# Zero matmuls in TensorE's early gaps, expert numbers read earlier, rows sent a turn sooner, result loads from two queues

## What is computed

```python
x = x + attention(layernorm(x), ln1_g, ln1_b, Wq, Wkv, Wo, ln2_g, ln2_b)   # x: (4, 512, 128)
x = x + experts(layernorm(x), gate_w, gate_up_w, down_w)

# attention: 16 query heads of 64, one key and one value head that all share
xn = layernorm(x) * ln1_g + ln1_b
q, k, v = xn @ Wq, xn @ Wk, xn @ Wv
attn = softmax(q @ k.T * 64 ** -0.5)
y = layernorm(concat_heads(attn @ v) @ Wo) * ln2_g + ln2_b

# experts: 8 of them, the best 2 of each token, 512 hidden features
probs = softmax(x @ gate_w.T);  topw, sel = top_k(probs, 2);  topw = topw / sum(topw)
out = sum over the 2 chosen e of  topw[e] * ((up_e(x) * gelu(gate_e(x))) @ down_w[e].T)
```

## Time and profile before

| | |
|---|---|
| median of 3 runs | 633.98 us (633.31 to 635.54) |
| the profiled execution, its own time | 634.79 us |
| its span, first to last instruction | 633.0 us |
| TensorE busy with matmuls | 575.8 us, 91% |
| VectorE busy | 422.4 us, 67% |
| GpSimd busy | 391.3 us, 62% |
| ScalarE busy | 303.7 us, 48% |
| mean granted clock of TensorE | 0.965 |

### The profile page before, as it was taken

The page is one execution under the profiler, slowest core; times in us unless marked ns, Lnnn a source line. Parts: engine busy times, 40 slices in busy tenths (PEclk is TensorE's granted clock), DMA queues, the critical chain, the costliest instruction groups (busy, mean ns, idle before and its releaser), DMA issues. The chain is left out here.

```text
span 633.0 us, 8708 instructions
## 1 busy us (share of the span) xinstructions
PE 575.8 (91%) x2559; PEld 324.4 (51%) x2559; DVE 422.4 (67%) x815; ACT 303.7 (48%) x570; POOL 391.3 (62%) x319
## 2 busy tenths in 40 slices
PE   2799999999999999979999989899997989899990
PEld 1354454444554454445544544444442567788880
DVE  3777558658847978686587767977485868344433
ACT  2235655445545554354556434355544654455540
POOL 4338686658668855598597556959755934355330
PEclk9889999999999999789999978999998999999995
DMA  6121011010101100061000000000006200231005
GB/s 173 47 88 69 2 68 69 0 69 0 70 16 53 69 1 1 5 250 47 1 1 1 2 1 15 17 6 0 10 1 167 64 22 27 53 97 36 21 14 199
DMA packets 23980, 29.28 MB, mean 46 GB/s; under 512 B 4403, under 2 KB 14901, under 8 KB 23936
## 3 DMA queue, kind: packets, MB, share of 16 engines
q1 hardware_dynamic: 21664, 24.50, 11.9%
q0 software_dynamic: 2272, 4.24, 2.0%
HBM read 13.73 MB, written 15.32 MB: 46 GB/s over the span
## 5 line engine op out<-in xcount | busy, mean ns | idle before, releaser
L1059 ACT ACTIVATE prob<-s_ps 128x512 f32<-128x512 f32 x256 | 150.6, 598 | 191.5 <-PE s_ps L1152 189.5
L985 DVE TENSOR_REDUCE rowmax<-max_ps 128x1 f32<-128x512 f32 x256 | 173.1, 685 | 90.1 <-PE max_ps L1121 88.4
L922 POOL TENSOR_TENSOR fold<-prob 128x1024 f32<-128x1024 f32 x63 | 149.6, 2374 | 96.7 <-ACT prob L1059 96.2
L1166 PE MATMUL pv_ps<-prob,v 128*64 128x512 f32 x512 | 140.4, 628 | 0.0
L1150 PE MATMUL s_ps<-q_hl,khh 128*128 128x512 f32 x256 | 119.3, 466 | 1.5 <-DMA q_hm<-mrow 0.9
L1121 PE MATMUL max_ps<-khh,q_hl 128*128 128x512 f32 x256 | 106.0, 422 | 9.0 <-DVE q_hl L974 4.4
L1152 PE MATMUL s_ps<-q_hm,kly 65*128 65x512 f32 x256 | 102.9, 402 | 0.0
L1150 PEld LDWEIGHTS s_ps<-q_hl,khh 128*128 128x128 f32 x256 | 49.3, 193 | 81.7 <-ACT prob L1059 58.1
L928 POOL TENSOR_TENSOR psums<-fold 128x512 f32<-128x512 f32 x63 | 81.3, 1290 | 4.9
L1121 PEld LDWEIGHTS max_ps<-khh,q_hl 128*128 128x128 f32 x256 | 50.4, 197 | 30.0 <-DVE rowmax L985 10.4
L1152 PEld LDWEIGHTS s_ps<-q_hm,kly 65*128 65x128 f32 x256 | 49.4, 193 | 9.1 <-issue 3.3
(11 more groups left out here) (218 smaller groups left out, 769.9 us busy)
## 6 DMA issues: line engine op xcount, KB each, us to landing
sorted_rows<-raw_w SPq DMA_DIRECT2D x36, 260.0 KB, 2.6
raw_w<-in_gate_upT SPq DMA_DIRECT2D x8, 512.0 KB, 7.6
wd<-in_downT SPq DMA_DIRECT2D x8, 256.0 KB, 4.2
raw_w<-parts SPq DMA_DIRECT2D x8, 256.0 KB, 4.0
psums<-sorted_rows SPq DMA_DIRECT2D x22, 65.0 KB, 1.8
x<-in_x SPq DMA_DIRECT2D x4, 256.0 KB, 5.3
out<-x SPq DMA_DIRECT2D x4, 256.0 KB, 2.7
xs_first<-sorted_rows SPq DMA_DIRECT2D x15, 65.0 KB, 1.9
```

The source lines that it names most:

```text
L922: nc.gpsimd.tensor_tensor(fold[:, :, :], prob[:, head % 4, 0:2, :], prob[:, head % 4, 2:4, :], ALU.add).then_inc(prob_folded, 1)
L985: nc.vector.tensor_reduce(rowmax[:, group % 2, it, i:i + 1], max_ps[:, k % 2, :], AX_X, ALU.max).then_inc(max_done, 1)
L1059: nc.scalar.activation(prob[:, head % 4, jt, :], s_ps[:, k % 2, :], ACT.Exp, scale=SCALE).then_inc(exp_done, 1)
L1166: last = nc.tensor.matmul(pv_ps[DH * hd:DH * hd + DH, :], v[:, b % 2, jt, :], prob[:, head % 4, jt, :], start=(jt == 0), stop=(jt == JT - 1))
```

## The change

Four things are changed.

- **Zeros.** A tile of zeros is cleared by GpSimd as its first step (in the last slot of `q_hm`, which is not used until later), and TensorE multiplies it by itself into `y_ps`, which nobody reads then, at fixed places of the first steps: 20 times at the very start, before the first K 8, before the first MAX 5, before the first EXP 3, before the first V 3, and once before each of the MAX tiles 2 to 11. None of these is followed by a signal.
- **Expert numbers.** TensorE's first three register loads stand ahead of the last row sum in the first block instead of behind the first transpose of the second.
- **Rows.** `SEND_AT` is 9 instead of 10, the turn in which PLACE stands.
- **Result loads.** SyncE issues four of the eight loads, and ScalarE, at the end of its program, the other four; each waits for all results first.

```diff
@@ -130,6 +130,10 @@
+BUSY = {"start": 20, "K": 8, "MAX": 5, "EXP": 3, "V": 3, "rows": 1}
 def shifts(units):
@@ -152,6 +156,9 @@
 EARLY_ROWS = 2
+OPEN = 3
@@ -276,6 +283,7 @@
         half_set = sem("half_set")
+        idle_set = sem("idle_set")
         x1_in = [sem(f"x1_in{b}") for b in range(NB)]
@@ -646,6 +654,12 @@
+        tile_expert = []
+        def load_expert(pe, k):
+            tile_expert.append(pe.value_load(tile_at[0:1, 0, k:k + 1], min_val=0, max_val=E - 1))
         def load_gate_up(sp, e):
@@ -793,6 +807,9 @@
+            idle_rows = q_hm[:, Q_SLOTS - 1, :]
             wq_raw = prob[:, 0, 0:2, :].rearrange("p a s -> p (a s)")
@@ -861,6 +878,7 @@
             def _(pool):
+                nc.gpsimd.memset(idle_rows.bitcast(F32), 0.0).then_inc(idle_set, 1)
                 nc.gpsimd.memset(minus_half[:, :], -0.5).then_inc(half_set, 1)
@@ -1077,10 +1095,20 @@
+                def keep_busy(times):
+                    for _ in range(times):
+                        nc.tensor.matmul(y_ps[:, :], idle_rows[:, 0:P], idle_rows, start=True, stop=True)
+                pe.wait_ge(idle_set, 1)
+                keep_busy(BUSY["start"])
                 pe.wait_ge(consts_in, 96)
                     b = u // 2
+                    if u == 0 and a == 0 and kind in BUSY:
+                        keep_busy(BUSY[kind])
                     if kind in ("XT", "K", "V", "Q", "SHIFT", "YT", "X3T", "LOGIT", "RANK") and (kind, u) != ("K", 0):
@@ -1115,6 +1143,8 @@
                             pe.wait_ge(q_lo, u * UH + i + 1)
+                        if 2 <= k < 12:
+                            keep_busy(BUSY["rows"])
                         if k >= 2:
@@ -1168,6 +1198,11 @@
                             last.then_inc(pv_mm, 1)
+                    if (kind, u, a) == ("SUM", last_unit, 1):
+                        pe.wait_ge(tiles_ready, 1)
+                        for k in range(OPEN):
+                            load_expert(pe, k)
                     tail_tensor(pe, kind, u, a)
@@ -1215,16 +1250,14 @@
-
-            OPEN = 3
             BETWEEN = {"YT": 3, "YSTAT": 3, "YADD": 4, "XSTAT": 4, "XNORM": 5, "X3T": 6, "LOGIT": 6, "CHOOSE0": 6, "CHOOSE1": 7,
-            SEND_AT = 10
+            SEND_AT = 9
             ROW_SENDS = range(SEND_AT, SEND_AT + TOP_K * TPB * 2 // 3 + 1)
-            assert SEND_AT > BETWEEN["PLACE"] and EOW >= TOP_K * TPB + 4
+            assert SEND_AT >= BETWEEN["PLACE"] and EOW >= TOP_K * TPB + 4
@@ -1259,6 +1292,14 @@
                 eng.wait_ge(parts_sent[k % EOW], 16 * (k // EOW + 1))
+            def load_parts(eng, n):
+                for k in range(NT - EOW, NT):
+                    sent(eng, k)
+                for b in range(NB):
+                    eng.dma_start(part_in[:, b, n, :, :], parts[n * T + b * S:n * T + (b + 1) * S, :].rearrange(
+                        "(p t) d -> p t d", t=TPB)).then_inc(parts_in[b], 16)
@@ -1280,12 +1321,7 @@
                         load_rows(sp, k, rows(k))
-                for k in range(NT - EOW, NT):
-                    sent(sp, k)
-                for b in range(NB):
-                    for n in range(TOP_K):
-                        sp.dma_start(part_in[:, b, n, :, :], parts[n * T + b * S:n * T + (b + 1) * S, :].rearrange(
-                            "(p t) d -> p t d", t=TPB)).then_inc(parts_in[b], 16)
+                load_parts(sp, 0)
                 for b in range(NB):
@@ -1435,6 +1471,8 @@
+                load_parts(act, 1)
             @block2.tensor
@@ -1494,10 +1532,6 @@
-                def expert(k):
-
-                    tile_expert.append(pe.value_load(tile_at[0:1, 0, k:k + 1], min_val=0, max_val=E - 1))
-
                 def gate(k):
@@ -1515,10 +1549,7 @@
-                tile_expert = []
                 turn_in(0)
-                for k in range(OPEN):
-                    expert(k)
                 for e in range(E):
```

## The result

The changed kernel takes 629.69 us (median of 20 runs, 623.06 to 635.11) against 634.84 (20 runs, 631.76 to 636.23): 5.1 us or 0.8% less. The prediction said 625.7 with a range of 621.8 to 630.2. The runs of the change spread over 12 us, those of before over 4.5. The profiled execution, 635.11 us with a span of 633.1, is the longest of the 20: its rows show what happened in it, and its total is not typical.

A forecast was written before the change was run, and what follows sets the result against it. No single engine fills the span: attention hands tiles between four engines, TensorE paces the experts' part. Terms 3.1 + 1.0 + 1.0 + 2.9 + 0.3 = 8.3 us gave a 625.7 us median, range 621.8 to 630.2.

The forecast's parts named there:

- part 2: Start of the experts' part: early register loads save TensorE 3.4 us, but GpSimd's late reciprocal leaves 1.0 us.
- rivals of 628.6 and 628.8: Start gives only 1 us and the 42 us spell stays (628.8), or part 3's wait moves (628.6); together chance 0.2.
- the first rival: GpSimd not in the way in part 2, or issue time counts in part 4: 2 us more, 623.5; chance 0.15.
- The fourth rival: Slower: clock falls come elsewhere later; two new spells take back 8.3 us, three give 641; chance 0.04.
- Part 1: Kernel start: zero matmuls raise TensorE's clock early, 3.1 us by the first exponential, plus 1.0 us at the later spell.
- the spell at 42: Attention, near the first values: a stretch at 0.57 of full clock that three zeros should remove, taken as 1.0 us.
- Without the 0.83: Before GpSimd's low halves: its 0.83 us wait for ScalarE disappears, so its reciprocal ends near 504.9.
- the forecast's own mechanism: Experts' part, after GpSimd's low halves: VectorE stands still 2 us for GpSimd's late reciprocal deviation, delaying TensorE's next down product.
- Part 3: Experts' turns: rows sent a turn sooner remove TensorE's wait for the last list's first tile, 2.9 us.
- Part 4: End of kernel: loading results from two queues saves only the second load's issue, 0.3 us, since bytes set the pace.

The follow-up runs named there:

- e5: The changed kernel with the three expert-number register loads back in the second block, leaving zeros, rows and result loads: 625.80 us, ratio 0.985.
- e3: The kernel before with only the row sends a turn sooner (SEND_AT 9 instead of 10): 635.28 us, ratio 1.001.
- e2: The kernel before with only the three expert-number register loads moved ahead of the last row sum: 642.40 us, ratio 1.012.
- e7: The changed kernel with five more zero matmuls ahead of the first query product: 628.69 us, ratio 0.991.
- e11: e5 with more zero matmuls at the key product, query product and row maxima: 623.69 us, ratio 0.981.
- e6: The changed kernel with one column cleared by GpSimd ahead of each of its eight low halves: 630.44 us, ratio 0.989.
- e9: The changed kernel with GpSimd told to wait for VectorE's third normalisation before its low halves: 623.42 us, ratio 0.982.
- e12: The changed kernel with e11's zeros and GpSimd waiting for VectorE's third hidden tile before its low halves: 624.64 us, ratio 0.984.
- e8: The changed kernel with VectorE's second low half moved ahead of its second normalisation: 627.23 us, ratio 0.988.
- e4: The kernel before with only the result loads issued from two queues: 635.55 us, ratio 1.001.
- e1: The kernel before with only the 49 zero matmuls added: 629.63 us, ratio 0.990.
- e10: e5 with GpSimd told to wait for VectorE's first low half before its own low halves: 625.69 us, ratio 0.984.

## Why the prediction was right and wrong

**The total** was in the range, 4 us above the value, and partly by luck: part 2 failed by 4.9 us, and the others gave 1.7 more than forecast. It is near the rivals of 628.6 and 628.8, but came by neither of their mechanisms. Three small sums of the prediction do not come out: the first rival is 625.7 - 2 = 623.7 and not 623.5, the range's upper end by its own rule 628.8 + 1.7 = 630.5 and not 630.2, and the chances in the list add up to 0.91 for faster and 0.04 for slower, not 0.92 and 0.03. None of them changes what follows. The fourth rival was set aside because spells are "a property of the program more than of the moment". For the kernel before that held (20 runs within 4.5 us), for the kernels with zeros it did not. The terms:

**Part 1, zeros: right in mechanism, both sizes off.** The matmuls came at the upper level within the first 20, from the eleventh on in the changed kernel and the eighth in e5. The first row sum is 2.7 us earlier in the changed kernel and 2.9 to 4.2 in the others with zeros, against 4.1 forecast (3.1 and 1.0). Of that the start gave less than 3.1: the first exponential's scores came 0.96 earlier in the changed kernel and 1.35 to 2.45 in the others. The rest, 1.3 to 1.7 instead of 1.0, came after that, and the spell at 42 is gone in all of them. What was missed is the rest of attention. The prediction counted one spell, that at 42 us. Kernels without zeros had 20 to 27 us of low clock before the last row sum; those with zeros 0 to 24. The last row sum moves from 464.2 at none to 473.7 at 20.5: (473.70 - 464.22) / 20.5 = 0.46 us for each us at low clock. At equal low clock the zeros win 476.81 - 473.70 = 3.1 (20.5, e3 and the changed kernel) and 476.69 - 474.17 = 2.5 (23.9, e2 and e5). So in these profiles they are worth about 3 us in any case and up to 9 more when the later spells are gone; that this makes most of the spread of the runs is argued from it and from their clocks, 0.965 to 0.982. What decides it is open: neither the idle time before the query product (e7) nor denser zeros (e11, 623.69 with 0.971 to 0.983, against 625.80 for e5, whose intervals overlap) settled it.

**Part 2, expert numbers: the step that failed.** It said that of 3.4 us on TensorE 1.0 is left, because GpSimd needs 13.12 us for its low halves and its reciprocal is then 2 us late. Of the 3.4 the wait held, 2.0 us sooner to the first gate product in every profile with early numbers. The products at full clock came in five of these seven profiles (1.8 us, e6 to e9 and e12) and not in the changed kernel and e2 (3.5). What failed is the step behind it, that GpSimd and VectorE would go on sharing as before. "Without the 0.83" was the sentence to stop at: the early numbers abolish that wait of GpSimd for ScalarE, and in all fourteen profiles GpSimd's sharing with VectorE goes with an idle time at that place. In the six without one GpSimd's row ran in 9.9 to 10.1 us and VectorE lost 7.6 to 9.6 us on one low half. The part costs 3.9 us by the medians (629.69 against 625.80; 2.9 by the ratios) and 7.4 alone, in e2, where the second low half is held as in the profiled execution of the changed kernel. The Trainium skill, SBUF — State Buffer, section "SBUF: two separate sides", says that a VectorE operation with two SBUF inputs and a GpSimd operation that reads SBUF exclude each other for a whole instruction. The trace agrees that they exclude each other (GpSimd's pieces of 1.25 become 2.28 when they yield), and shows more: VectorE lost to six (e8) or seven instructions in a row. In e12, with turns taken again, the forecast's own mechanism appears: the variance is ready at 491.17 + 0.48 = 491.65 and GpSimd's reciprocal starts at 495.28, 3.6 later; VectorE idles 1.51 us for it, where 2 were forecast. e12 is no faster than e11, which has the numbers late; its ScalarE stop of 3.0 us, in a turn of 5.25 (3.56 in e11), may hide a gain of 1 to 2 us. So whether the early numbers are worth the forecast 1.0 once nobody is held stays open.

**Part 3, rows: right for the turn.** 2.9 forecast; the turn fell from 5.77 to 2.8 and the experts' part of e5 is 138.1 - 135.2 = 2.9 shorter. Alone it was worth nothing over 12 runs of e3. In the one profiled, ScalarE's stop and the slow turn behind it took 1.7 + 1.5 us; that the other runs lose it the same way is not shown.

**Part 4, loads: nearly right.** 0.3 forecast, 0.0 in the trace and nothing in e4.

**Sum.** In e5 the parts without the numbers give 634.85 - 625.80 = 9.0 by the medians, against 3.1 + 1.0 + 2.9 + 0.3 = 7.3. The whole change gave 634.84 - 629.69 = 5.1 of the 8.3: part 2 brought -3.9 instead of +1.0, 4.9 less, and the others these 1.7 more. The other 0.9 of the 4.0 us by which the forecast was low is the kernel before, whose median over 20 runs is 634.84 and not the 633.98 of three.

## What to carry to other kernels

When a change abolishes a short wait, ask what else goes with that wait: here the profiles without 0.8 us of idle time on GpSimd have an experts' part longer by 2 to 7 us. Test each part of a bundle alone and left out: alone, the rows looked worth nothing and the numbers cost 7 us; in the bundle the rows' turn was 2.9 us shorter, and the numbers were the part to drop. Of the versions run, the changed kernel without the early numbers and with denser zeros (623.69, ratio 0.981) beats both kernels; e9 (623.42, 0.982) and e12 (624.64, 0.984), which keep the numbers, cannot be told from it.

## What the hardware did that was not expected

- Two engines that take turns on subtractions over the same tiles can fall into a state in which one is kept out for the rest of the other's row: up to 9.6 us for a 1.22 us operation, six profiles; in eight others, with GpSimd idle 0.56 to 1.71 us beforehand, at most 2.31.
- A cleared column between two subtractions of GpSimd does not end that state (e6, 9.53).
- With zeros in TensorE's early gaps, the spells at half clock that otherwise stood between 250 and 384 us were gone in some executions (e1, e8) and there in others (e5, e10) of nearly the same program: 464.2 against 474.2 at the last row sum.
- ScalarE stopped for 1.0 to 3.0 us around the rows' sends in five of the profiles, with its input ready, for a releaser that the view does not name.
